# Running layer 0 of the next sequence beside the last layers of this one, in one block of an eight-layer kernel

## Chip, cores and metric

The kernel runs on one core of a Trainium2 chip. The metric is the device time of one execution in microseconds (us), taken as the median of several runs. TensorE is called PE here, VectorE DVE, ScalarE ACT, GpSimd POOL and SyncE SP; SP issues the DMAs.

## The reference

A float32 input of 8 sequences of 512 tokens with 128 features goes through eight residual layers, each on the layer norm of x:

```
x += mamba(ln(x))          # layer 0: silu(conv), x_proj, delta = softplus(...), both directions
                           # h = exp(delta*A)*h + delta*xc*B ;  y = sum_n h*C   (16 states n, 256 channels)
x += moe0(ln(x))           # 16 experts, grouped top-2, silu
x += attn1(ln(x)); x += lora1(ln(x)); x += attn2(ln(x))
x += block2(ln(x))         # attention, then ln, 8 experts of 512 with gelu, then ln
x += memory(ln(x))         # F = ret*F + coef*(v k^T) ;  y = (W_LTM + F) q, 8 groups of 128 rows
x += moe3(ln(x))           # 8 experts of 256: silu(h1)*h3, top-2 of softmax gates
```

A "sequence" is one pass over one of the 8 rows of the batch; all the weights stay in SBUF.

## The kernel before

`Fori(0, 8)` loops over the sequences. Its body is a row of stages, and each stage is one or more blocks. In a block every engine has its own in-order instruction list, with semaphores between the lists; at a block's end all engines meet. `norm_tiles` is a block of its own in front of each stage. SP clears the semaphores of finished stages in the next norm block, and those of the loop's last stage in a block of its own behind it.

Mamba has two blocks behind its norms. The first (the "pre" part) makes the projections, the convolutions (DVE), silu, delta by Abs, Exp and Ln (ACT), and the three-part bf16 rows `bcs` of B and C. The second is the scan: 32 steps (2 directions of 16 states), each over two tiles of channels at once, 1024 columns. In step s PE spreads the row of B over 128 partitions (L835), DVE multiplies it by `du` (L893) and one step later runs the scan (L900), ACT writes the decays into PSUM (L872) and copies the spread row of C (L878), POOL multiplies by C (L926), and PE adds the product of step s-4 into the accumulator with four matmul instructions (L849). DVE may not start the product of step s before that accumulation: `if s >= RW: dve.wait_ge(acc, s - RW + 1)`. The scan's PSUM use is 4 banks of decays, 2 of accumulators and 2 of spread rows.

`block2` ends in the experts of 512 (32 tiles of 128 hidden features: one up product, L1463, a gelu, L1488, one down product, L1454, and at each fourth tile `weigh`, L1502). They go round in 4 banks. `moe3` has 16 tiles; a tile has an up product (L1463), a gate product (L1465), a silu on ACT (L1492), one multiplication on DVE (L1512), and a down product. Up and gate products have two banks each. `memory` makes q, k and v parts, and then runs 8 groups, each with an outer product (L1692), a scan (L1694) and a read-out (L1700) on DVE, over two sets of three banks. `gates` makes the router's top-2 weights on DVE; its bank is `PS[7]`.

## Time and profile before

| what | us |
|---|---|
| median of 3 runs | 6054.27 |
| lowest and highest | 6046.32, 6057.73 |
| profiled execution, its own time | 6033.15 |
| span of that execution | 6031.4 |
| mean granted TensorE clock | 0.844 |
| busy: PE, DVE, ACT, POOL | 4418.4, 3707.3, 2786.1, 1094.8 |
| start of the second pass, start of the third | 798.66, 1546.12 |

A busy share of the whole span is a mean over stages with different limits, so it must be read stage by stage. The second pass of the loop, from 798.7 to 1546.1 us, is used for that. Durations of instructions in the rows are in us; the idle time of an engine before an instruction and what ended it stand in square brackets behind it.

### The profile page before, as it was taken

To read this page: it belongs to the slowest core of one execution; us is meant where nothing else is said; L and a number is where in the kernel's file an instruction comes from. 1 tells how busy PE (TensorE), PEld (TensorE's weight loads), DVE (VectorE), ACT (ScalarE), POOL (GpSimd) and SP (SyncE) were. 2 spreads that over 40 slices of the span, in tenths; PEclk is the share of its full clock that TensorE was granted. 3 is DMA by queue.
4 is the path that set the end of the run, shared out by engine and by line. 5 is a ranking of instruction groups with operands and counts; after the bars stand their busy time and mean duration, and the time that the engine had idled before them with its cause. 6 is when DMAs were issued, how large, how long until landed. Compare 5 with 4: busy or idle time off the path is not lost. (4 is left out here: it accounts for less than half of the span.)

```text
span 6031.4 us, 66197 instructions
## 1 busy us (share of the span) xinstructions
PE 4418.4 (73%) x20516; PEld 2189.1 (36%) x20516; DVE 3707.3 (61%) x8373; ACT 2786.1 (46%) x5281; POOL 1094.8 (18%) x1100
## 2 busy tenths in 40 slices
PE   5787767877678775787758877587775877758777
PEld 2342423424234242342424424243342433414334
DVE  6756477564775647756476554765548655486554
ACT  3455334553445534455344553455534555345553
POOL 2301033010330103301032010320104201042100
PEclk8987889878898788987889878898788987889778
DMA  2000000000000000000000000000000100001000
GB/s 109 19 31 1 2 3 25 25 1 2 3 25 25 1 2 3 31 19 1 2 3 31 19 1 2 3 31 19 1 2 3 37 13 1 2 3 37 13 1 4
DMA packets 30363, 84.02 MB, mean 14 GB/s; under 512 B 2640, under 2 KB 11856, under 8 KB 29440
## 3 DMA queue, kind: packets, MB, share of 16 engines
q1 hardware_dynamic: 29968, 79.30, 4.1%
q8 instruction: 182, 2.98, 0.2%
q14 instruction: 213, 1.74, 0.1%
HBM read 77.12 MB, written 2.16 MB: 13 GB/s over the span
## 5 line engine op out<-in xcount | busy, mean ns | idle before, releaser
L167 POOL TENSOR_TENSOR rstd<-rstd,WF 128x4 f32<-128x4 f32 x88 | 88.9, 1010 | 3692.8 <-DVE rstd L185 3005.2
L926 POOL TENSOR_TENSOR mamba_work<-mamba_work,mamba_c_all 128x1024 f32<-128x1024 f32 x256 | 602.4, 2354 | 324.6 <-DVE mamba_work L900 324.6
L900 DVE TENSOR_TENSOR_SCAN mamba_work<-BANKS,mamba_work 128x1024 f32<-128x1024 f32 x256 | 582.6, 2278 | 0.0
L835 PE MATMUL BANKS<-mamba_bcs,WB 96*128 96x512 bf16 x512 | 207.1, 414 | 427.2 <-DVE mamba_work L893 317.9
L849 PE MATMUL BANKS<-mamba_work,WF 128*128 128x512 f32 x1024 | 495.7, 607 | 17.5 <-POOL mamba_work L926 17.5
L1463 PE MATMUL BANKS<-XT,WF 128*128 128x512 f32 x768 | 418.5, 630 | 0.0
L1232 DVE CUSTOM_DVE_ANT_0 attn_biased<-BANKS,attn_toep 128x512 f32<-128x512 f32 x512 | 350.4, 685 | 55.0 <-DMA attn_toep<-bias_line 38.1
L1211 ACT COPY attn_probt<-BANKS 128x512 f32<-128x512 f32 x512 | 298.6, 583 | 168.3 <-PE BANKS L1137 165.3
L1203 ACT ACTIVATE attn_prob<-attn_biased,attn_nmax 128x512 f32<-128x512 f32 x512 | 373.7, 730 | 1.5 <-DVE attn_nmax L1232 1.4
L513 DVE TENSOR_REDUCE inner_nmax<-BANKS 128x1 f32<-128x512 f32 x512 | 322.5, 684 | 73.9 <-PE BANKS L386 71.3
L878 ACT COPY mamba_c_all<-BANKS 128x512 f32<-128x512 f32 x256 | 150.1, 586 | 428.7 <-PE BANKS L835 414.0
L893 DVE TENSOR_TENSOR mamba_work<-BANKS,mamba_du 128x1024 f32<-128x1024 f32 x256 | 313.0, 1223 | 40.1 <-PE BANKS L849 13.5
L872 ACT ACTIVATE BANKS<-mamba_delta,WF 128x511 f32<-128x511 f32 x512 | 334.0, 689 | 6.1 <-DVE mamba_work L900 6.0
L224 ACT COPY XT<-BANKS 128x256 f32<-128x256 f32 x64 | 23.8, 373 | 676.4 <-PE BANKS L216 676.4
L1137 PE MATMUL BANKS<-WF,attn_prob 128*128 128x128 f32 x2048 | 320.5, 281 | 8.8 <-ACT attn_probt L1211 4.9
L1137 PEld LDWEIGHTS BANKS<-WF,attn_prob 128*128 128x128 f32 x2048 | 218.4, 140 | 278.9 <-DVE attn_prob L1239 179.6
L1454 PEld LDWEIGHTS BANKS<-WF,block_a 128*128 128x128 f32 x2048 | 273.2, 195 | 124.3 <-issue 114.7
L510 DVE CUSTOM_DVE_ANT_0 attn_masked<-BANKS,WF 128x384 f32<-128x384 f32 (+3 forms) x512 | 231.1, 489 | 139.4 <-PE BANKS L386 138.4
L1502 DVE SCALAR_TENSOR_TENSOR block_Y<-BANKS,block_comb,block_Y 128x128 f32<-128x128 f32 x256 | 72.1, 344 | 380.0 <-PE BANKS L1454 380.0
L1488 ACT ACTIVATE block_a<-BANKS,WF 128x512 f32<-128x512 f32 x256 | 176.0, 687 | 264.9 <-PE BANKS L1463 264.8
L1130 PE MATMUL BANKS<-attn_qk 64*128 64x512 f32 x1024 | 289.0, 641 | 5.4 <-ACT attn_qk L1185 5.4
L835 PEld LDWEIGHTS BANKS<-mamba_bcs,WB 96*128 96x128 bf16 x512 | 48.5, 99 | 670.8 <-DVE mamba_work L893 497.2
(412 smaller groups left out, 9142.6 us busy)
## 6 DMA issues: line engine op xcount, KB each, us to landing
attn_toep<-bias_line SPq DMA_DIRECT2D x128, 448.0 KB, 4.4
WF<-in_wf SPq DMA_DIRECT2D x4, 1964.0 KB, 16.2
WF<-in_wf SPq DMA_DIRECT2D x3, 800.0 KB, 16.1
WF<-in_wf SPq DMA_DIRECT2D x3, 785.5 KB, 5.9
XIN<-in_x SPq DMA_DIRECT2D x9, 256.0 KB, 4.0
out<-X SPq DMA_DIRECT2D x8, 256.0 KB, 2.4
WF<-in_wf SPq DMA_DIRECT2D x1, 799.5 KB, 19.0
WF<-in_wf SPq DMA_DIRECT2D x1, 784.5 KB, 9.7
```

What stands on the lines that cost most here:

```text
L513: V.tensor_reduce(nmax[:, j, h:h + 1], bank("S", s), AX.X, ALU.max, negate=True).then_inc(maxed, 1)
L849: last = nc.tensor.matmul(PS[ACC + t][:, :], ident, work[:, m % RW, t, :], start=(n == 0), stop=(n == NS - 1))
L872: last = nc.scalar.activation(decay[m % RD][:, t, 1:], delta[:, d, t, 1:], ACT.Exp, scale=W("A")[:, a:a + 1])
L893: V.tensor_tensor(work[:, s % RW, :, :], bc(PS[SPREAD].unsqueeze(1), [P, ND, SEQ]), du[:, s // NS, :, :], ALU.mult).then_inc(drv, 1)
L900: V.tensor_tensor_scan(w, decay[m % RD].rearrange("p t s -> p (t s)"), w, 0.0, ALU.mult, ALU.add).then_inc(scn, 1)
L926: nc.gpsimd.tensor_tensor(work[:, m % RW, :, :], work[:, m % RW, :, :], bc(c_all[:, m % 2, :].unsqueeze(1), [P, ND, SEQ]), ALU.mult).then_ ...
L1130: nc.tensor.matmul(PS[(s + a) % NS_], q[:, j * P:(j + 1) * P], k, start=True, stop=True).then_inc(scored, 1)
L1137: last = nc.tensor.transpose(bank[:, kt * P:(kt + 1) * P], prob[:, u % NP_, kt * P:(kt + 1) * P], ident)
L1203: nc.scalar.activation(prob[:, e % NP_, :], biased[:, e % NS_, :], ACT.Exp, bias=nmax[:, e:e + 1], scale=-1.0, accum_out=den[:, e:e + 1]). ...
L1211: nc.scalar.copy(probt[:, u % NT_, :], RING[n % 2]).then_inc(freed, 1)
L1232: V.tensor_tensor_reduce(biased[:, s % NS_, :], PS[s % NS_], toep[:, h % 4, c:c + SEQ], -1.0, BIG, ALU.add, ALU.min, nmax[:, s:s + 1]).the ...
L1463: last = nc.tensor.matmul(PS[i % NB][:, :], w_up[:, i * P:(i + 1) * P], XT[:, :], start=True, stop=True)
```

## The change

The loop body starts with layer 1. Layer 0 of the first sequence runs alone ahead of the loop (stage `first`). In passes 1 to 7 the block `slot` runs layer 0 of the next sequence beside the second half of block2 (its norm and experts), memory and moe3 of this one; the last sequence is written out behind the loop, without a companion. Mamba has banks 0 to 3 and the three layers banks 4 to 7. Each layer is a Python generator for each engine: before a piece of work it yields the time in a plan at which that piece is due, and `in_turn` writes the pieces of both streams into one engine's list in the order of the due times. At run time only this order remains.

```
def in_turn(*streams):
    due = [next(s, None) for s in streams]
    while any(t is not None for t in due):
        i = min((t, i) for i, t in enumerate(due) if t is not None)[1]
        due[i] = next(streams[i], None)
```

Due times of mamba: pre part from 13.5, scan step s at `49.0 + 3.6*s` on PE, its tile t on DVE at `49.6 + 3.6*(s + t/2)`, its decays on ACT at `45.4 + 3.6*s`, the end from 164.2. Due times of the others: tile i of the experts of 512 at `7.6 + 2.0*i` (its gelu 1.0 later, the down product of tile i-1 also 1.0 later), second norm 73, norm of memory 79, memory 84 and its group g at `102 + 3.2*g`, norm of moe3 131, its tile i at `136.7 + 3.0*i`, the last piece at 187.7.

```diff
 # mamba scan, DVE (one step was: product of 1024 columns, then the scan of 1024 of the step before)
+                    if i:
+                        dve.wait_ge(scn, i)
+                    V.tensor_tensor(DRIVE, SPREAD, du[:, d, t, :], ALU.mult).then_inc(drv, 1)
+                    dve.wait_ge(drv, i + 1)
+                    dve.wait_ge(dec, i + 1)
+                    V.tensor_tensor_scan(work[:, s % RW, t, :], decay[:, s % RD, t, :], DRIVE, 0.0,
+                                         ALU.mult, ALU.add).then_inc(scn, 1)
 # C: rows go to DRAM once, and each step a DMA spreads one row
-                            spread(1, s - 1).then_inc(c_cast, 1)
-                        nc.scalar.copy(c_all[:, m % 2, :], PS[SPREAD + 1][:, :]).then_inc(c_cp, 1)
+                sp.dma_start(c_dram[d], rows_bc[NS:2 * NS, d, :]).then_inc(cput, 16)
+                if m >= RC:
+                    sp.wait_ge(rd, m - RC + 1)
+                src = bass.AP(row.tensor, row.offset, [[0, P], [1, SEQ]])
+                sp.dma_start(c_all[:, m % RC, :], src).then_inc(c_ld[m % RC], 16)
 # mamba pre part, ACT: both halves of softplus come off the bank, which the two directions share
+                nc.scalar.activation(soft[:, d, :, :], BANKS[:, 2:4, :], ACT.Abs).then_inc(ab, 1)
+                nc.scalar.activation(delta[:, d, :, :], BANKS[:, 2:4, :], ACT.Relu).then_inc(relued, 1)
 # mamba pre part, PE: the second direction
+                    pe.wait_ge(relued, 1)
 # moe3: silu(u)*g = (tanh(u/2)+1) * g/2 * u; up and gate products take turns in two banks
-                            nc.scalar.activation(s1[:, i % 2, :], PS[i % NB][:, :], func, bias=b_up[:, i:i + 1]).then_inc(acted, 1)
-            V.scalar_tensor_tensor(a1[:, i % 3, :], PS[2 + i % NB][:, :], b_gate[:, i:i + 1], s1[:, i % 2, :],
+                    nc.scalar.activation(s1[:, i % 2, :], UP[slot["up", i] % 2], ACT.Tanh, bias=half[:, i:i + 1],
+                                         scale=0.5).then_inc(acted, 1)
+                    act.wait_ge(hid, 2 * i + 2)
+                    nc.scalar.activation(g1[:, i % 2, :], UP[slot["gate", i] % 2], ACT.Identity, bias=half[:, n + i:n + i + 1],
+                                         scale=0.5).then_inc(gate_off, 1)
+                    link(V.scalar_tensor_tensor(s1[:, i % 2, :], s1[:, i % 2, :], 1.0, g1[:, i % 2, :], ALU.add, ALU.mult))
+                    V.scalar_tensor_tensor(a1[:, i % 3, :], UP[slot["up", i] % 2], b_up[:, i:i + 1], s1[:, i % 2, :],
+                                           ALU.add, ALU.mult).then_inc(gated, 1)
 # the loop
-    with nc.Fori(0, out.shape[0]) as b:
+    with Stage("first", last=True) as st:
+        layer = mamba(st)
+        with nc.Block() as block:
+            run(block, layer)
+        with Stage("slot", last=True, at_end=store) as st:
+            taken = st.sem("x_taken")
+            streams = [mamba(st, after=(taken, 1))] if ahead else []
+            streams.append(last_layers(st, taken))
+    with nc.Fori(0, out.shape[0] - 1) as b:
+        layers(b, True)
+    layers(out.shape[0] - 1, False)
```

Memory's groups have one set of three banks in place of two, and the experts of 512 two banks in place of four. Up product i of moe3 waits for the multiplication of tile i-1, which reads the bank. The slot has 123 semaphores (47 of mamba), cleared in a block behind it. The four middle stages and the first half of block2 stay.

## Rows read from the trace of the kernel before

**Rows 1.** Windows of pass two: us, busy us of PE, PEld, DVE, ACT, POOL; clock, DMA.

```profile
798.70:844.70 46.00, 21.18 (x37) 6.42 (x37) 32.43 (x65) 18.10 (x22) 8.20 (x8) 0.69 0.00 1
844.70:959.60 114.90, 73.66 (x183) 26.96 (x183) 110.54 (x66) 58.04 (x97) 74.41 (x32) 0.94 0.00 0
959.60:973.50 13.90, 7.75 (x24) 4.84 (x24) 5.01 (x8) 0.00 (x0) 2.50 (x2) 0.76 0.00 0
973.50:1356.20 382.70, 304.87 (x1644) 141.71 (x1644) 228.41 (x684) 213.51 (x456) 47.79 (x93) 0.83 0.06 20
1356.20:1427.30 71.10, 63.10 (x344) 45.75 (x344) 17.98 (x65) 24.34 (x36) 1.02 (x1) 0.93 0.00 1
1427.30:1438.80 11.50, 1.24 (x4) 0.75 (x5) 7.58 (x30) 0.37 (x1) 2.01 (x2) 0.51 0.00 1
1438.80:1457.40 18.60, 10.21 (x57) 6.89 (x58) 10.23 (x21) 11.85 (x18) 0.00 (x0) 0.66 0.00 1
1457.40:1484.90 27.50, 17.45 (x48) 6.66 (x48) 21.50 (x26) 6.80 (x10) 0.00 (x0) 0.89 0.00 0
1484.90:1540.00 55.10, 49.12 (x216) 31.05 (x216) 27.60 (x78) 14.62 (x21) 1.01 (x1) 0.90 0.02 6
1540.00:1546.10 6.10, 0.00 (x0) 0.00 (x0) 0.00 (x0) 0.00 (x0) 0.00 (x0) 0.52 0.17 51
```

**Rows 2.** Timeline of one scan step: start, us, engine, line, operation.

```profile
903.74 1.22 DVE L893 TENSOR_TENSOR mamba_work<-BANKS,mamba_du 128x1024 f32<-128x1024 f32 x1
904.88 2.28 DVE L900 TENSOR_TENSOR_SCAN mamba_work<-BANKS,mamba_work 128x1024 f32<-128x1024 f32 x1
905.02 0.39 PE L835 MATMUL BANKS<-mamba_bcs,WB 96*128 96x512 bf16 x1 [1.17 <-DVE mamba_work L893]
905.25 1.88 PE L849 MATMUL BANKS<-mamba_work,WF 128*128 128x512 f32 x4
...
907.24 1.22 DVE L893 TENSOR_TENSOR mamba_work<-BANKS,mamba_du 128x1024 f32<-128x1024 f32 x1
```

**Rows 3.** Timeline of one group of memory on DVE.

```profile
1461.48 0.68 DVE L1692 TENSOR_TENSOR memory_heb<-BANKS,memory_vrc 128x512 f32<-128x512 f32 x1
...
1462.20 1.23 DVE L1694 TENSOR_TENSOR_SCAN memory_mem<-WF,memory_heb 128x512 f32<-128x512 f32 x1
...
1463.46 0.75 DVE L1700 SCALAR_TENSOR_TENSOR memory_red<-memory_mem,WF,BANKS 128x512 f32<-128x512 f32 x1
```

**Rows 4.** Timeline of one tile of the experts of 512, on PE.

```profile
1406.26 1.05 PE L1454 MATMUL BANKS<-WF,block_a 128*128 128x128 f32 x8
...
1407.15 1.02 PE L1463 MATMUL BANKS<-XT,WF 128*128 128x512 f32 x2
...
1408.01 1.05 PE L1454 MATMUL BANKS<-WF,block_a 128*128 128x128 f32 x8
```

**Rows 5.** Timeline of moe3 on ACT, two tiles.

```profile
1505.63 0.69 ACT L1492 ACTIVATE moe_s<-BANKS,WF 128x512 f32<-128x512 f32 x1 [2.34 <-PE BANKS L1465]
...
1508.24 0.69 ACT L1492 ACTIVATE moe_s<-BANKS,WF 128x512 f32<-128x512 f32 x1 [1.92 <-PE BANKS L1465]
```

**Rows 6.** Timeline of ACT at the first gelu, behind the router's exponent.

```profile
1366.07 1.28 ACT L1488 ACT_TABLE_LOAD   x1
1367.36 0.69 ACT L1488 ACTIVATE block_a<-BANKS,WF 128x512 f32<-128x512 f32 x1
```

**Rows 7.** Timeline of ACT in the first stage: an Exp, then a Tanh.

```profile
47.41 0.19 ACT L671 ACTIVATE WF<-init_m_c 128x8 f32<-128x8 f32 x1
47.51 0.19 ACT L672 ACTIVATE init_m_t<-init_m_t 128x8 f32<-128x8 f32 x1
```

**Rows 8.** Timeline: the Abs of mamba's pre part.

```profile
826.71 1.01 ACT L754 ACTIVATE mamba_soft<-BANKS 128x1024 f32<-128x1024 f32 x1
```

**Rows 9.** The clearing line on SP, at moe0's norm and at the loop's end.

```profile
L143 SPq EVENT_SEMAPHORE_RANGE_CLEAR  x42: 25/30/35, 973.3 to 976.1; - x42
...
L143 SPq EVENT_SEMAPHORE_RANGE_CLEAR  x19: 25/30/37, 1540.6 to 1542.1; - x19
```

**Rows 10.** The page's DMA issues: KB each, median us to landing.

```profile
attn_toep<-bias_line SPq DMA_DIRECT2D x128, 448.0 KB, 4.4
```

More of the change, by code:

```diff
@@ L135, in clear_stale, with _ @@
     def clear_stale(block, first=lambda sp: None):
-        if stale:
-            @block.sync
-            def _(sp):
-                first(sp)
-                for stage in stale:
-                    for s in stage.sems:
-                        sp.sem_clear(s)
+        @block.sync
+        def _(sp):
+            first(sp)
+            for stage in stale:
+                for s in stage.sems:
+                    sp.sem_clear(s)
     def release_stale():
@@ L287, in weights @@
             beside(0)
+            yield 3.0
             score = ex
@@ L323, in gates @@
         pieces.products, pieces.turn, pieces.exponents, pieces.move, pieces.weights = products, turn, exponents, move, weights
-        pieces.combed, pieces.moved = combed, moved
+        pieces.combed, pieces.moved, pieces.shifted = combed, moved, shifted
         return pieces
@@ new lines, in run, with _ @@
+    def run(block, *streams, first=lambda sp: None):
+        @block.sync
+        def _(sp):
+            first(sp)
+            in_turn(*(p.sync(sp) for p in streams if "sync" in p.engines))
+        @block.tensor
+        def _(pe):
+            in_turn(*(p.tensor(pe) for p in streams))
+        @block.scalar
+        def _(act):
+            in_turn(*(p.scalar(act) for p in streams))
+        @block.gpsimd
+        def _(pool):
+            in_turn(*(p.gpsimd(pool) for p in streams))
+        @block.vector
+        def _(dve):
+            in_turn(*(p.vector(dve) for p in streams))
@@ L930, in bass_mk_seq, with layers, load_next @@
+    with Stage("first", last=True) as st:
+        layer = mamba(st)
+        with nc.Block() as block:
+            run(block, layer)
+    def layers(b, ahead):
+        def load_next(sp):
+            sp.wait_ge(x_free, 16)
+            sp.sem_clear(x_free)
+            sp.sem_clear(xin_ld)
+            if ahead:
+                sp.dma_start(XIN[:, :, :], one(xs, b + 1)).then_inc(xin_ld, 16)
         with Stage("moe0") as st:
-            norm_tiles(st, "ln", X, XN, XT)
+            norm_tiles(st, "ln", X, XN, XT, beside=load_next)
@@ L1008, in _ @@
                     V = nc.vector
-                    gate.weights(dve)
+                    for _ in gate.weights(dve):
+                        pass
                     link = Chain(dve, pch)
@@ L1273, in _ @@
                 def _(dve):
-                    gate.weights(dve)
+                    for _ in gate.weights(dve):
+                        pass
                     link = Chain(dve, ch)
@@ L1706, in store @@
-        def store(sp):
-            sp.dma_start(one(ys, b), X[:, :, :]).then_inc(x_free, 16)
-            sp.wait_ge(loaded, 16)
-        with Stage("moe3", last=True, at_end=store) as st:
-            loaded = st.sem("loaded")
-            def load_next(sp):
-                sp.dma_start(XIN[:, :, :], one(xs, b + 1)).then_inc(loaded, 16)
-            norm_tiles(st, "ln", X, XN, XT)
-            comb, comb_t = st.sb("comb", [P, NJ, E3]), st.sb("comb_t", [E3, SEQ])
-            gate = gates(st, XT, W("Wg3"), E3, comb, comb_t, eps=0.0)
-            experts(st, gate, W("W1_3"), W("W3_3"), W("b1_3"), W("b3_3"), W("W2_3"), W("b2_3", E3), E3, HID // P, ACT.Silu,
-                    comb, comb_t, X, load=load_next)
+        with Stage("attn3") as st:
+            norm_tiles(st, "ln", X, XN, XT)
+            O = st.sb("O", [P, NJ, D])
+            rope_attention(st, W("qkv3"), W("bqkv3"), True, False, O)
+            project_back(st, "pb", O, W("o3"), XN, bias=W("bo3"))
@@ new lines, in store, with clear @@
+        def store(sp):
+            sp.dma_start(one(ys, b), XO[:, :, :]).then_inc(x_free, 16)
+        def clear(sp):
+            for stage in stale:
+                for s in stage.sems:
+                    sp.sem_clear(s)
+        with Stage("slot", last=True, at_end=store) as st:
+            taken = st.sem("x_taken")
+            streams = [mamba(st, after=(taken, 1))] if ahead else []
+            streams.append(last_layers(st, taken))
+            with nc.Block() as block:
+                run(block, *streams, first=clear)
+            release_stale()
```

1197 lines of the change are left out of this document (709 added, 488 removed).

## The prediction

> **What bounds the kernel now.** I read the windows of the second pass first [rows 1], because the page's shares (PE 73%, DVE 61%) hide that the stages are bound in turn. The reader is to see that mamba's scan is DVE's (110.5 of 114.9 us), the experts of 512 and moe3 are PE's (63.1 of 71.1, 49.1 of 55.1), memory's groups are DVE's (21.5 of 27.5), and the rest is latency: in mamba's pre part DVE is busy for 32.4 of 46.0 us, in its tail (13.9) and in the norms (11.5) nobody is. Outside the middle stages (382.7) a pass takes 174.8 (mamba) + 183.8 (the three layers) + 6.1 (store, clearing, jump) = 364.7 us, and 8 of them are 2917.6. Then I read single steps in the timeline [rows 2 to 6] for the loops that come back in another form.
>
> **The room.** Beside each other the streams ask of DVE: mamba without its scan window 148.0 - 110.5 = 37.5; the scan as 64 pairs of product and scan of 512 columns. Such a pair stands in [rows 3]: from the outer product to the read-out 1.98, so 126.7. The three layers' DVE rows [rows 1] add up to 84.9, and moe3's second multiplication, priced as the read-out (0.75), adds 16 x 0.75 = 12. With 1.4 for emptying the accumulator that is 262 us against 358.6 in series. PE has 243.7 busy in the same rows, less 32 spreads of 0.39, much of it at a clock of 0.69. So DVE is the floor.
>
> **Part 1, layer 0 alone, once.** In the old step the accumulation is hidden: from the product's end (904.96) over spread and accumulation to the next product (907.24) is 2.28, the time of the scan [rows 2]. Now the wait starts at the second half's product, and only its scan of 1.26 covers it. A step is 1.98 + 0.70 + 2.28 = 4.96; the first four accumulate nothing and take 3.96; emptying costs 2. So 4 x 3.96 + 28 x 4.96 + 2 = 156.7 for 114.9, +42. Relu of 1024 columns (as Abs, 1.01 [rows 8]) lies partly on the pre part's path: +1. 174.8 + 43 = 217.8.
>
> **Part 2, three layers alone, once.** A tile of moe3 takes 2.61 [rows 5]. Now up product i waits for the multiplication of tile i-1: product 1.02 [rows 4], Tanh 0.69, Identity 0.69, two operations of DVE 1.5, five hand-offs together 0.35: 4.25. Fifteen tiles cost 15 x 1.64 = +24.6, and the router's comparisons, which now lie in that loop, +3. The experts of 512 keep PE's 1.75 per tile [rows 4] with two banks, since a gelu of 0.69 ends under the down product of 1.05. Memory +1, blocks merged -3. 183.8 + 25.6 = 209.4.
>
> **Part 3, clearing.** 42 clears took 2.8 us and 19 took 1.5 [rows 9], about 66 ns each. The slot's 123 lie between two blocks where nothing runs: 8.1 for 1.5, so an end of 12.7 for 6.1. The first stage has 47 (+3.1), the last 76 (end 9.9).
>
> **Part 4, C by DMA.** It takes 32 spreads (0.39 of PE) and 32 copies off ACT, neither of which was on the path, and puts 256 KB on SP's queue each step. Nothing here shows a spreading DMA; the nearest, 448 KB, lands in 4.4 us [rows 10], the small end is about nothing. The buffer is free two steps ahead, 8 to 10 us less POOL's 2.4, so I price it at 0; beyond 5 to 7 us it would be waited for. The decays written to SBUF and the product written to PSUM I take at the old durations.
>
> **Part 5, the slot.** I wrote down each engine's order from the due times and walked through it with the durations above, each piece starting when its engine is free and its last input is there. The four stretches:
>
> A, up to the first scan step: 84 us. The pre part alone has 46.0, and 20 of 32 tiles of the experts should ride along (20 x 1.75 = 35, below 46). But ACT must do both streams in one list. The list alternates exponent, gelu, silu, gelu, silu, gelu, silu, gelu, exponent, logarithm, gelu: at each change of function the trace has a load of 1.28 with nothing behind it [rows 6]. Additions to 46.0: +10 up to the last convolution (the inner norm's transposes stand on PE behind the first down product, which waits for the first gelu; DVE waits in the first `weigh` for the fourth down product); +13 to its silu (it stands on ACT behind the forward rows and gelus 8 to 11, and gelu 8 behind the forward rows of mamba; PE meanwhile waits in down product 8); +7 to the deltas (x_proj of the second direction waits for the Relu, which stands behind gelu 13, as the two directions share banks 2 and 3); +8 to the first product (two Relus, loads, and down product 19 stands before the first spread while its gelu stands behind decays that wait for delta). In series these parts took 46.0 plus about 46 for the norm and 20 tiles. So almost nothing is won. Unknown here is whether silu and gelu need a load between them, since the trace never has one behind the other: without it six loads (8 us of ACT) go, half of them in a chain, so A lies between 79 and 90 with PE's clock at the lower level for part of it.
>
> B, from there to memory's norm: 64 us for 9.5 steps and 12 tiles, in series 33 + 21 + 11.5 = 66. While gelus and decays alternate, a step needs of ACT 2 x 1.28 + 2 x 0.65 + 1.8 x 0.69 = 5.2, and the down product waiting for a gelu stands before the next spread: about 6 us a step.
>
> C, memory: 110 us for 14 steps, the 46.1 of its rows and a norm. DVE has 28 pairs (55.4) and 38 more; 17 are waits, of which 5.4 where PE stands in the wait for the last total's copy (ACT) with the next spread behind it, 3 where the first step waits behind memory's projections, 2 at the emptied accumulator. In series this was 14 x 3.5 + 46.1 + 5 = 100: DVE was nearly full in both parts before, and the pairs of 1.98 and the waits are added to it.
>
> D, moe3 with 8 steps and mamba's tail: 98 us. DVE has 16 pairs (31.7), 39.6 of moe3 and 5 of the tail. The tile loop of 4.25 and the step loop of 4.96 go through the same PE list, so a step in a tile's way costs both. The bad case: the multiplication of tile i-1 ends at 0; DVE goes on with a pair (its product ends at 0.7); PE does up and gate product of tile i until 1.9 and only then spread and accumulation, until 4.0; DVE's next pair runs from 4.1 to 6.1, and only behind it, in the order of the list, the two multiplications of tile i, ready since 2.8, until 7.6. In the good case the spread falls behind the down product and a tile takes 5.5, without a step 4.3. Seven tiles run behind the scan's end, the tail between them, at 4.25 and the tail's pieces, 38 us. In series D was 8 x 3.5 + 13.9 + 55.1 = 97.
>
> S = 84 + 64 + 110 + 98 = 356, as good as the 358.6 in series.
>
> **Sum.** Outside the middle: 217.8 + 3.1 + 209.4 + 9.9 + 7 x (S + 12.7) = 529.1 + 7 S, against 2917.6. Break-even is S = 341.2. With 356: +103.5. The profiled execution took 6033.15 (span 6031.4), which gives 6137; the median of the three runs lies 21 above it, 6054.27, so the forecast is 6158.
>
> One rule bears on it. The Trainium skill, "ScalarE: Activation LUTs", section "What ACT_TABLE_LOAD costs", gives 1.28 us for a load and 1.38 of drain behind it, and section "Rules for kernel authors" asks to do all of one table set before switching. The trace agrees with the load and not with the drain: the gelu starts 0.01 us after the load's end [rows 6]. With the page's drain the 27 loads of stretches A and B would cost 37 us more of ACT per slot.
> The page also has Exp and Tanh in one set ("Table sets: the hidden batching unit"), and the trace agrees, as no load stands between them [rows 7].
>
> **Rivals.** (1) The streams do fill each other's gaps, and the slot is the DVE floor with a start and an end that are half idle: 262 + about 50 = 312, that is -205, 5850. For it: in each stretch the three other engines are half idle; it decides below S = 341. Against it: my walk, and the single banks DRIVE, VB, KB and QB. It ends on the other side. (2) The waits feed on each other more than in a walk without any jitter, or PE's clock falls in its waits (0.69 in the old pre part, 0.94 in the scan [rows 1]): S = 385, +306, 6360. (3) Each change of function costs ACT more than its load, such as a wait for the pipe to empty before it. From the rows the gap is 0.01; doubled loads, of which some 23 lie in a chain, would give S = 385 too, 6360. (4) The gains of some stretches and the once-only costs cancel: S = 341 +- 2, 6054. (5) The change doesn't do what it says: the streams stand in series because one list waits for the other all through, S = 359 + 47 (steps) + 26 (moe3) = 432, +635.
>
> **How the numbers follow.** Forecast (S 344 to 372, 6073 to 6270): 0.50. Rival 1 (S 280 to 339): 0.28. Rival 2: 0.12. Rival 3: 0.03. Rival 4: 0.05. Rival 5: 0.02. About 0.2%, 12 us, is what a measurement of this kernel tells from no change, and S 339.5 to 343 is that. Faster 0.29, same 0.04, slower 0.67. To hold 8 in 10 the range takes in the forecast, the upper part of rival 1 (S from 325, -114) and rival 2 up to S = 385: 5940 to 6330, a little less than its end. The forecast's own range is 6073 to 6270.
>
> **What the profile should show.** From the slot's first norm to its last add about 356 us, DVE busy for about 260 of them (0.73); the first scan product 84 us after its start; 30 table loads in a slot, 9 in a pass before; single-stream steps of 4.96 in the stage ahead of the loop and moe3 tiles of 4.25 behind it; 123 clears in about 8 us; no wait for the DMAs of C. I am wrong if the slot is shorter than 341, and then I expect the error in stretch A, where the order is worst by my walk, or in D. A wait of POOL for C, or a product into PSUM over 0.7, would lengthen every step.

## The result, and the profile after

The changed kernel takes 6340.19 us (median of 4 runs, 6334.26 to 6347.79), the kernel before on the same chip 6052.22: a ratio of 1.0477, 95% interval 1.0459 to 1.0495. It is slower, as forecast, but by 288 us where the forecast had 104, and its time lies above the end of the range (6330). The profiled execution took 6347.79 us (span 6346.1, mean granted clock 0.820 for 0.844).

Windows of the changed kernel: the stage where layer 0 runs alone; 98.3 us of its scan; the first half of the first pass (the four middle stages and the first half of block2); then the first slot in the four stretches A, B, C, D of the prediction, and the whole of it; last, the last pass's three layers. A ends at the slot's first scan product, B at the last copy of memory's norm, C at the last copy of moe3's norm, in this kernel and in all the edits of it. Columns as in [rows 1].

```profile
51.10:324.80 273.70, 144.66 (x212) 49.02 (x212) 163.80 (x201) 62.83 (x89) 85.08 (x40) 0.60 0.10 31
101.70:200.00 98.30, 50.94 (x67) 16.66 (x68) 61.36 (x65) 23.90 (x36) 39.34 (x17) 0.53 0.16 46
324.80:711.90 387.10, 310.10 (x1644) 143.24 (x1644) 228.37 (x683) 213.40 (x456) 47.68 (x93) 0.82 0.07 21
...
711.90:796.10 84.20, 60.95 (x256) 36.53 (x257) 46.93 (x113) 48.66 (x62) 10.83 (x9) 0.88 0.03 8
796.10:858.20 62.10, 41.85 (x163) 23.67 (x162) 48.01 (x85) 38.33 (x46) 23.22 (x11) 0.83 0.13 38
858.20:982.60 124.40, 71.62 (x181) 31.06 (x182) 100.08 (x121) 38.88 (x57) 34.64 (x16) 0.79 0.09 30
982.60:1085.50 102.90, 75.67 (x282) 41.88 (x281) 74.57 (x119) 31.33 (x49) 21.78 (x9) 0.95 0.06 18
711.90:1085.50 373.60, 250.10 (x880) 133.15 (x880) 269.59 (x437) 157.20 (x211) 90.47 (x44) 0.86 0.08 23
...
6124.90:6340.20 215.30, 147.27 (x668) 93.14 (x668) 96.43 (x236) 68.03 (x100) 4.04 (x4) 0.85 0.00 0
```

The reader is to see three things. A (84.2) and B (62.1) came out as forecast (84, 64); C and D did not (124.4 for 110, 102.9 for 98). The seven slots take 373.6, 370.6, 373.5, 370.2, 370.6, 373.5 and 373.6, 372.2 on the mean, so a difference of 3 us in one slot says little. The first stage, which occurs once, is 273.7 us for a forecast of 217.8 + 3.1. And the first half of the pass, whose code the change leaves alone, has the 1644 matmuls of [rows 1] at 310.1 us of busy PE for 304.9.

A scan step of the first stage, in the timeline (answers to [rows 2]). The whole step, from one first product to the next, is 188.65 - 181.79 = 6.86 us. Most of the 28 steps that accumulate have this length; the next one, in which the accumulation takes 2.54, has 5.60.

```profile
181.79 0.70 DVE L899 TENSOR_TENSOR BANKS<-BANKS,first_du 128x512 f32<-128x512 f32 x1 [2.92 <-PE BANKS L745]
182.53 1.22 DVE L902 TENSOR_TENSOR_SCAN first_work<-first_decay,BANKS 128x512 f32<-128x512 f32 x1
183.78 0.70 DVE L899 TENSOR_TENSOR BANKS<-BANKS,first_du 128x512 f32<-128x512 f32 x1
184.52 1.22 DVE L902 TENSOR_TENSOR_SCAN first_work<-first_decay,BANKS 128x512 f32<-128x512 f32 x1
184.54 0.61 PE L735 MATMUL BANKS<-first_bcs,WB 96*128 96x512 bf16 x1 [2.84 <-DVE BANKS L899]
184.94 3.62 PE L745 MATMUL BANKS<-first_work,WF 128*128 128x512 f32 x4
188.65 0.70 DVE L899 TENSOR_TENSOR BANKS<-BANKS,first_du 128x512 f32<-128x512 f32 x1 [2.92 <-PE BANKS L745]
```

DVE's part is as forecast (product 0.70, scan 1.22). The four accumulating matmuls take 3.62 us where [rows 2] has 1.88: TensorE runs at its lower level of 1.2 GHz. The window says the same: a granted clock of 0.53.

The end of a slot, the clearing line on SP (answers to [rows 9]), and the page's DMA issues for C (the nearest rows were [rows 10]):

```profile
L149 SPq EVENT_SEMAPHORE_RANGE_CLEAR  x123: 25/30/43, 1086.6 to 1094.0; - x123
```

```profile
slot_c_all<-c_rows SPq DMA_DIRECT2D x224, 256.0 KB, 3.1
```

What ended DVE's waits in the slot, in the list of waits: us in total, times, longest.

```profile
DVE BANKS L899 <- PE BANKS L745: 34.5, 14, 8.8
DVE slot_bcs L863 <- ACT slot_rows_bc L762: 11.5, 2, 8.7
DVE slot_x_s L1044 <- ACT slot_x_g L1023: 9.8, 6, 2.9
DVE BANKS L899 <- PE BANKS L735: 8.3, 2, 6.0
DVE slot_Y L1033 <- PE BANKS L973: 7.9, 2, 7.1
```

The largest item is the scan's product waiting for PE, with the accumulation (L745) just ahead of its release. No wait names a DMA of C.

A group of memory in the slot (answers to [rows 3]), with POOL's multiplication beside it:

```profile
902.68 0.67 DVE L1234 TENSOR_TENSOR slot_heb<-BANKS,slot_vrc 128x512 f32<-128x512 f32 x1
...
902.84 2.35 POOL L829 TENSOR_TENSOR slot_work<-slot_work,slot_c_all 128x1024 f32<-128x1024 f32 x1 [3.95 <-DVE slot_work L902]
...
903.38 2.90 DVE L1238 TENSOR_TENSOR_SCAN slot_mem<-WF,slot_heb 128x512 f32<-128x512 f32 x1
```

Memory's scan, 1.23 in [rows 3], takes 2.90 here: it starts 0.54 us behind POOL's instruction, POOL ends at 905.19, and 1.1 us later, at 906.28, the scan is over. Mamba's scan (L902), which reads one operand from PSUM, takes 1.22 beside POOL as well.

### The profile page after: what moved, and what is told of

Read it like the earlier page. It is cut to its first block and busy times, and to the rows that moved or that the text cites. A ratio compares the mean times of both kernels' runs of the same rounds, so it can differ in the third digit from the quotient of the medians.

```text
span 6346.1 us, 66283 instructions
## 1 busy us (share of the span) xinstructions
PE 4553.8 (72%) x20260; PEld 2242.5 (35%) x20260; DVE 3996.1 (63%) x9013; ACT 2945.0 (46%) x5323; POOL 1102.1 (17%) x1100
## 5 line engine op out<-in xcount | busy, mean ns | idle before, releaser
L829 POOL TENSOR_TENSOR slot_work<-slot_work,slot_c_all 128x1024 f32<-128x1024 f32 x224 | 536.5, 2395 | 1199.0 <-DVE slot_work L902 1199.0
L808 ACT ACTIVATE slot_decay<-slot_delta,WF 128x512 f32<-128x512 f32 x448 | 298.8, 714 | 658.9 <-DVE slot_work L902 633.6
L902 DVE TENSOR_TENSOR_SCAN slot_work<-slot_decay,BANKS 128x512 f32<-128x512 f32 x448 | 546.6, 1220 | 15.3
L745 PE MATMUL BANKS<-slot_work,WF 128*128 128x512 f32 x896 | 539.4, 736 | 20.4 <-DVE slot_du L908 20.4
L899 DVE TENSOR_TENSOR BANKS<-BANKS,slot_du 128x512 f32<-128x512 f32 x448 | 310.6, 693 | 324.2 <-PE BANKS L745 233.2
L973 PEld LDWEIGHTS BANKS<-WF,slot_x_a 128*128 128x128 f32 x2688 | 368.4, 201 | 269.2 <-ACT slot_x_a L1015 142.1
L495 ACT ACTIVATE attn_prob<-BANKS 128x512 f32<-128x512 f32 (+3 forms) x896 | 401.1, 532 | 129.0 <-PE BANKS L397 125.2
L973 PE MATMUL BANKS<-WF,slot_x_a 128*128 128x128 f32 x2688 | 381.7, 288 | 86.1 <-ACT slot_x_a L1015 86.1
L397 PE MATMUL BANKS<-attn_parts_kT,attn_parts_qT 64*128 64x512 bf16 (+3 forms) x896 | 314.2, 444 | 32.6 <-ACT attn_parts_qT L475 20.7
L524 DVE TENSOR_REDUCE attn_nmax<-BANKS 128x1 f32<-128x512 f32 x448 | 282.0, 683 | 71.2 <-PE BANKS L397 68.9
L745 PEld LDWEIGHTS BANKS<-slot_work,WF 128*128 128x128 f32 x896 | 208.7, 235 | 195.7 <-issue 184.4
```

The source lines that it names most:

```text
L397: nc.tensor.matmul(bank(kind, i), left[rows, P * tile:P * (tile + 1)], right[rows, lo:hi], start=True, stop=True).then_inc(sem, 1)
L495: nc.scalar.activation(prob[:, i % PR, lo:hi], bank("T", i), ACT.Exp).then_inc(exped, 1)
L745: last = nc.tensor.matmul(PS[t][:, :], ident, work[:, m % RW, t, :], start=(n == 0), stop=(n == NS - 1))
L808: nc.scalar.activation(decay[:, m % RD, t, :], delta[:, d, t, :], ACT.Exp, scale=W("A")[:, a:a + 1]).then_inc(dec, 1)
L829: nc.gpsimd.tensor_tensor(work[:, m % RW, :, :], work[:, m % RW, :, :], bc(c_all[:, m % RC, :].unsqueeze(1), [P, ND, SEQ]), ALU.mult).then ...
L899: V.tensor_tensor(DRIVE, SPREAD, du[:, d, t, :], ALU.mult).then_inc(drv, 1)
```

## The experiments

All are edits of the changed kernel (6340) unless said otherwise. The slot and its stretches are of the first pass, except where the mean of the seven slots is given; a pass is the time from moe0's norm to that of the next sequence, 773.3 in the changed kernel's first pass. A single run is given without an interval. The kernel before took 6034 to 6055 beside them, so some 20 us of a difference between two single runs can be noise.

Slots in us, from the first statistics to the last addition:

| run | first slot | mean of seven |
|---|---|---|
| changed kernel | 373.6 | 372.2 |
| acc_first (2) | 355.5 | 355.5 |
| tables (4) | 363.4 | 363.8 |
| poolcut (5) | 367.7 | 368.1 |
| hebps (6) | 373.8 | 367.7 |
| yev (7) | 373.2 | 370.9 |
| silu (8) | 359.3 | 357.3 |
| combo (9) | 334.5 | 334.4 |
| combo_slow (10) | 333.9 | 335.0 |
| combo_fast (11) | 341.1 | 340.9 |
| zeros1, zeros2 (13, 14) | 373.1, 375.1 | 375.4, 375.9 |
| combo_zeros (15) | 339.7 | 339.1 |

**1. The streams in series.**

```diff
             with nc.Block() as block:
-                run(block, *streams, first=clear)
+                run(block, streams[-1], first=clear)
+            if ahead:
+                with nc.Block() as block:
+                    run(block, streams[0])
```

> Same instructions as the changed kernel, but the slot's two streams stand in two blocks one behind the other, the three layers first, mamba second. Theory (the overlap itself works, and the rewritten forms and the once-only parts eat it): the new forms cost alone what the stage ahead of the loop (273.7 us) and the last pass's three layers (215 us) take, so a slot grows from 371 to about 488 us, the run to about 6340 + 7 x 117 = 7160 us. Rival (the shared lists make the streams wait for each other so much that beside and behind each other cost the same): about 6340 us.

Measured: 7133.68. Windows of the three layers and of layer 0, first pass:

```profile
712.60:927.90 215.30, 147.78 (x668) 93.13 (x668) 96.25 (x236) 67.99 (x100) 4.05 (x4) 0.85 0.00 1
927.90:1197.90 270.00, 144.79 (x212) 48.99 (x212) 163.62 (x201) 62.84 (x89) 84.91 (x40) 0.58 0.10 31
```

In series the new forms need 485 us (215.3 + 270.0); one block brings them to 373.6. So the streams do overlap, by about 112 us a pass, and the fifth rival is out. But the old forms took 358.6 in series [rows 1]: the new forms cost 127 before they save anything, and 95 of that is layer 0 (270.0 for 174.8), at a clock of 0.58.

**2. The accumulation ahead of the spread.** The product of step s needs the spread of s, but not the accumulation of s-4.

```diff
 # the pieces cut at "..." are moved, not changed
             for s in range(STEPS + AHEAD):
-                yield SCAN + STEP * s if s < STEPS else TAIL + 1.0 + s - STEPS
+                m = s - AHEAD
+                if m >= 0:
+                    yield SCAN + STEP * s - 1.2 if s < STEPS else TAIL + 1.0 + s - STEPS
+                    ...                       # accumulation of step m
                 if s < STEPS:
+                    yield SCAN + STEP * s
                     ...                       # spread of step s
-                m = s - AHEAD
-                if m >= 0:
-                    ...                       # accumulation of step m
```

> The accumulation of step s-4 stands on PE ahead of the spread of step s (due 1.2 earlier), not behind it; nothing else changes. Theory (the path product, spread, four accumulating instructions, next product sets the step, and its waits let PE's clock fall): a step alone goes from 6.86 to about 4.0 us, the stage ahead of the loop from 274 to about 185, and of the 34.5 us that DVE waits for the accumulation in a slot some 25 go: 6340 - 88 - 175 = about 6080 us. Rival (in the slot the wait only moves to another piece of the lists): about 6250 us.

Measured: 6143.01, between the theory's 6080 and the rival's 6250. The first stage is 204 us (-69; the theory had 185), the step 4.08, the pass 756.1 (-17). Windows of the scan alone, then of A to D:

```profile
101.70:200.00 98.30, 55.41 (x104) 19.44 (x105) 88.65 (x94) 31.93 (x48) 54.10 (x23) 0.78 0.19 62
...
643.40:727.70 84.30, 61.18 (x256) 36.71 (x257) 46.90 (x113) 48.66 (x62) 10.83 (x9) 0.88 0.02 8
727.70:783.10 55.40, 41.72 (x164) 23.99 (x164) 48.60 (x86) 38.23 (x46) 23.25 (x11) 0.84 0.13 41
783.10:899.70 116.60, 69.38 (x183) 29.64 (x181) 99.52 (x121) 38.12 (x57) 34.64 (x16) 0.78 0.11 33
899.70:998.90 99.20, 75.59 (x279) 42.34 (x279) 73.71 (x120) 31.22 (x49) 21.76 (x9) 0.93 0.06 19
```

A stays. B loses 6.7, C 7.8 and D 3.7, although C now holds 15 steps for 14 (and D 7 for 8), and the clock is no higher in C and D (0.78 for 0.79, 0.93 for 0.95); so in the slot the gain is the order's. In the first stage order and clock come together: the clock is 0.78 for 0.53. The place of four matmuls in a list is worth 197 us, two thirds of the whole regression.

**3. TensorE kept busy in the first stage.** Two products behind each accumulation, into banks unused there. The other pieces of the edit, which pass `warm=True` to the first stage alone, are left out.

```diff
+                    if warm and s < STEPS:
+                        for k in range(2):
+                            nc.tensor.matmul(PS[6 + k], ident, W("early"), start=True, stop=True)
```

> In the stage ahead of the loop only, two float32 products of 512 columns into unused banks follow each accumulation, in the time in which PE would wait for the next product of DVE. Theory (the step of 6.86 us there, forecast at 4.96, is the forecast's path at half the clock): granted clock of the stage's scan from 0.56 to above 0.9, step about 5.0, stage 274 to about 218, the run 55 us shorter. Rival (the step is another chain, such as POOL or the DMA of C): stage unchanged or longer.

Measured: 6302.27, 38 us shorter where 55 were expected; the first stage is 227 us (-46), for 218. Window and step (the first product at 149.36 and 154.30):

```profile
101.70:200.00 98.30, 66.06 (x149) 26.32 (x150) 77.08 (x81) 28.16 (x43) 47.96 (x21) 0.90 0.18 56
```

```profile
152.10 0.39 PE L735 MATMUL BANKS<-first_bcs,WB 96*128 96x512 bf16 x1 [1.12 <-DVE BANKS L902]
...
152.33 1.88 PE L745 MATMUL BANKS<-first_work,WF 128*128 128x512 f32 x4
```

With more work PE is faster: clock 0.90, accumulation 1.88, step 4.94. That is the forecast's step of 4.96, so the order was priced rightly and the clock was not. What still lies above 217.8 is in part the emptied accumulator, whose step takes 9.23 in place of 4.95: 4.3 us for the 2 of the forecast.

**4. The gelu of the experts of 512 and the silus of mamba as Tanh.** The output changes; only the functions differ, so that table loads go. Both stand in the slot, and in the first stage and the last pass too.

```diff
-                nc.scalar.activation(zs[:, t, :], PS[ND + t][:, :], ACT.Silu).then_inc(zed, 1)
+                nc.scalar.activation(zs[:, t, :], PS[ND + t][:, :], ACT.Tanh).then_inc(zed, 1)
...
-                    nc.scalar.activation(xc[:, d, t, :], xc[:, d, t, :], ACT.Silu).then_inc(silu, 1)
+                    nc.scalar.activation(xc[:, d, t, :], xc[:, d, t, :], ACT.Tanh).then_inc(silu, 1)
...
-                    nc.scalar.activation(a1[:, i % 3, :], UP[slot["up", i] % 2], ACT.Gelu, bias=b_up[:, i:i + 1]).then_inc(acted, 1)
+                    nc.scalar.activation(a1[:, i % 3, :], UP[slot["up", i] % 2], ACT.Tanh, bias=b_up[:, i:i + 1]).then_inc(acted, 1)
```

> The gelu of the experts of 512 and the silus of mamba's pre part are Tanh (other values), so that they need no other table than Exp; the table loads in a slot fall from 30 to about 8. Theory (the loads lie in the chain of stretches A and B): both together shrink from 146 to about 128 us, the run to about 6340 - 7 x 18 = 6214 us. Rival (ACT has room beside PE and DVE there): within 12 us of 6340.

Measured: 6282.4, 58 us shorter for the theory's 126. The slot's table loads fall from 29 to 4, a pass is 763.7 (-9.6); A is 79.1 (-5.1), its ACT busy for 34.2 us in place of 48.7, as the window shows:

```profile
715.20:794.30 79.10, 61.69 (x255) 37.07 (x256) 46.93 (x113) 34.19 (x51) 10.83 (x9) 0.87 0.03 7
```

Loads count, but a third of ACT's saving arrives. The third rival, loads that cost double, would have put A far above 84.

**5. POOL multiplies 16 of 512 columns.** The output changes; POOL's instruction is all but gone.

```diff
-                nc.gpsimd.tensor_tensor(work[:, m % RW, :, :], work[:, m % RW, :, :],
-                                        bc(c_all[:, m % RC, :].unsqueeze(1), [P, ND, SEQ]), ALU.mult).then_inc(rd, 1)
+                nc.gpsimd.tensor_tensor(work[:, m % RW, :, 0:16], work[:, m % RW, :, 0:16],
+                                        bc(c_all[:, m % RC, 0:16].unsqueeze(1), [P, ND, 16]), ALU.mult).then_inc(rd, 1)
```

> POOL's product with C takes 16 columns of each tile in place of 512, so that most of y isn't multiplied by C; every wait stays. Theory (DVE operations with both operands in SBUF are held up while POOL multiplies in SBUF, as memory's scan, 1.22 us alone and 2.90 beside a product of POOL): DVE's busy time in a slot falls from 270 to about 250 us, memory's scan to 1.22 us, a slot by 12 to 18 us, the run to about 6340 - 105 = 6235 us. Rival (DVE's long operations come from something else, such as the DMAs of C): DVE's busy time unchanged, the run within 20 us of 6340.

Measured: 6312.23. Memory's scans, the slot's window and that of C:

```profile
L1238 DVE TENSOR_TENSOR_SCAN slot_mem<-WF,slot_heb x8: 1224/1224/1226, 903.0 to 954.5; 128x512 f32<-128x512 f32 x8
```

```profile
711.80:1079.50 367.70, 256.38 (x880) 137.16 (x880) 253.14 (x437) 157.19 (x211) 23.23 (x44) 0.82 0.08 23
858.40:978.30 119.90, 75.70 (x181) 33.23 (x182) 88.09 (x121) 38.81 (x57) 5.26 (x16) 0.71 0.10 31
```

In the changed kernel the same eight scans have a maximum of 2895 ns. With POOL gone DVE is busy for 253.1 in place of 269.6, so 16.5 us of DVE's busy time in a slot was waiting beside POOL. Twelve of them lie in C (88.1 for 100.1). The slot is only 5.9 shorter (4.1 on the mean of seven), and the expectation for the run was nearly four times as much. That speaks against DVE as the bound, but does not settle it: the clock fell as well (0.82 for 0.86 in the slot, 0.71 for 0.79 in C), and the same 181 matmuls of C took PE 4.1 us more, which can have hidden a part of the gain.

**6. Memory's outer product in place in PSUM**, so that its scan reads one operand from SBUF.

```diff
-                    pe.wait_ge(hd, g)
+                    pe.wait_ge(sd, g)
...
-                V.tensor_tensor(heb[:, :], KB, vrc[:, g % 2, :], ALU.mult).then_inc(hd, 1)
+                V.tensor_tensor(KB, KB, vrc[:, g % 2, :], ALU.mult).then_inc(hd, 1)
...
-                V.tensor_tensor_scan(mem[:, :], bc(W("ret")[:, g:g + 1], [P, SEQ]), heb[:, :], 0.0,
+                V.tensor_tensor_scan(mem[:, :], bc(W("ret")[:, g:g + 1], [P, SEQ]), KB, 0.0,
                                      ALU.mult, ALU.add).then_inc(sd, 1)
```

> Memory's outer product is written over its own PSUM bank, so that the scan reads one operand from PSUM, as mamba's does; PE's next product into that bank waits for the scan. Theory (both operands in SBUF): the scan has 1.22 us beside POOL too, 5 us less of DVE in a slot, the run 20 to 35 us shorter. Rival: the scan keeps its 1.85 us mean.

Measured: 6314.54. All eight scans take 1.22. The first slot is not shorter (373.8), the other six are, by 3.5 to 7 us. In the timeline the scan stands beside POOL's instruction (902.26 to 904.61):

```profile
902.80 1.22 DVE L1238 TENSOR_TENSOR_SCAN slot_mem<-WF,BANKS 128x512 f32<-128x512 f32 x1
```

**7. PE's wait for memory's last total 1.2 later in its list.**

```diff
             total(NG - 1)
+            yield G0 + STEP * NG + 1.2
             pe.wait_ge(yev, 1)
```

> PE's wait for the copy of memory's last total comes due 1.2 later, behind the next spread of mamba, not ahead of it. Theory (the wait of DVE for the accumulation there, 8.8 us in the first slot, is a wait behind a piece of the other stream): 6 us off a slot, the run 42 us shorter. Rival (memory's end is itself the chain): no change.

Measured: 6328.77. The spread now goes ahead, and DVE's longest wait falls from 8.8 to 6.0:

```profile
969.19 0.70 DVE L899 TENSOR_TENSOR BANKS<-BANKS,slot_du 128x512 f32<-128x512 f32 x1 [5.99 <-PE BANKS L745]
```

The first slot is only 0.4 us shorter (1.3 on the mean of seven), and the 11 us of the run are within the noise of single runs. Stretches C and D hold other waits of the same kind, and the time is given back there or in the order of the steps behind; where exactly was not located. A stall that the forecast had priced by itself (5.4) is not worth what it lasts.

**8. moe3 with Silu again:** one multiplication on DVE and no Identity on ACT, with the two banks as changed.

```diff
-                    nc.scalar.activation(s1[:, i % 2, :], UP[slot["up", i] % 2], ACT.Tanh, bias=half[:, i:i + 1],
-                                         scale=0.5).then_inc(acted, 1)
...
-                    nc.scalar.activation(g1[:, i % 2, :], UP[slot["gate", i] % 2], ACT.Identity, bias=half[:, n + i:n + i + 1],
-                                         scale=0.5).then_inc(gate_off, 1)
+                    nc.scalar.activation(s1[:, i % 2, :], UP[slot["up", i] % 2], ACT.Silu, bias=b_up[:, i:i + 1]).then_inc(acted, 1)
...
-                    link(V.scalar_tensor_tensor(s1[:, i % 2, :], s1[:, i % 2, :], 1.0, g1[:, i % 2, :], ALU.add, ALU.mult))
-                    V.scalar_tensor_tensor(a1[:, i % 3, :], UP[slot["up", i] % 2], b_up[:, i:i + 1], s1[:, i % 2, :],
+                    V.scalar_tensor_tensor(a1[:, i % 3, :], UP[slot["gate", i] % 2], b_gate[:, i:i + 1], s1[:, i % 2, :],
                                            ALU.add, ALU.mult).then_inc(gated, 1)
```

> moe3 with the Silu of ACT and one multiplication on DVE again, in two banks. The up bank is free after the Silu. Theory (the tile loop through two operations of ACT and two of DVE costs more than table loads): the last pass's three layers go from 215 to about 190 us, a slot loses 0 to 8 us although Silu and Exp take turns there, the run 25 to 80 us shorter. Rival (some 16 more table loads in a slot lie in the chain): the last pass gains the 25 us, a slot is longer by more than 5 us, the run longer than 6350 us.

Measured: 6209.31, more of a gain than expected. The last pass's three layers take 188 us for 215, the slot 359.3 for 373.6, although its table loads rise from 29 to 40. Stretch D alone falls from 102.9 to 85.7:

```profile
984.00:1069.70 85.70, 71.67 (x282) 40.22 (x281) 61.31 (x104) 35.14 (x44) 21.11 (x9) 0.99 0.07 22
```

The tile alone, in the timeline of the changed kernel and then of this one (answer to [rows 5]):

```profile
6292.09 0.69 ACT L1020 ACTIVATE zslot_x_s<-BANKS,HB 128x512 f32<-128x512 f32 x1 [2.79 <-PE BANKS L983]
...
6296.54 0.69 ACT L1020 ACTIVATE zslot_x_s<-BANKS,HB 128x512 f32<-128x512 f32 x1 [2.90 <-PE BANKS L983]
```

```profile
6169.31 0.69 ACT L1020 ACTIVATE zslot_x_s<-BANKS,WF 128x512 f32<-128x512 f32 x1 [1.92 <-PE BANKS L983]
6171.92 0.69 ACT L1020 ACTIVATE zslot_x_s<-BANKS,WF 128x512 f32<-128x512 f32 x1 [1.92 <-PE BANKS L983]
```

4.45 against 2.61: with Silu even two banks give the old tile. It is the Tanh form that holds a bank for two more operations.

**9. Edits 2, 6, 7 and 8 together** (combo), the one edit with more than one run.

> Four edits together on the changed kernel: the accumulation ahead of the spread in PE's list, moe3 with Silu and one multiplication, the wait for memory's last total 1.2 later in PE's list, and memory's outer product multiplied in place in PSUM. One by one they took 197, 131, 12 and 26 us off 6340. If they are independent the sum is 5975 (5950 to 6005), below the kernel before (6052): a slot of about 334 us, first stage 204, the last pass's three layers 188. Rival: the first two take the same waits of stretch D away (step and tile loop there share PE's list), so that together they bring at most the larger one in the slot: 6050 to 6080, no better than before.

Measured: 5972.28 (5971.14 to 5985.1) against 6034.4 of the kernel before: ratio 0.9902, interval 0.9885 to 0.9919. The first slot:

```profile
643.20:727.60 84.40, 61.24 (x256) 36.73 (x257) 46.98 (x114) 48.63 (x62) 10.82 (x9) 0.86 0.03 8
727.60:782.80 55.20, 41.47 (x164) 23.96 (x164) 48.55 (x86) 38.23 (x46) 23.21 (x11) 0.84 0.14 41
782.80:894.40 111.60, 68.07 (x183) 29.35 (x181) 94.71 (x122) 38.36 (x57) 34.64 (x16) 0.78 0.13 34
894.40:977.70 83.30, 71.90 (x279) 41.19 (x279) 61.24 (x103) 35.10 (x44) 21.07 (x9) 0.95 0.08 23
```

So the four mends make the change 1% faster than the kernel before, not slower. A slot is 334.5 us, below the forecast's break-even of 341.2. The four gains add up (197 + 131 + 11 + 26 = 365; measured 368), more closely than single runs can show. D is 20 us shorter than in the changed kernel.

**10 and 11. Combo with the scan steps due every 4.0 or every 3.3 us.**

> As combo, with mamba's scan steps due every 4.0 us in place of 3.6, so that more steps lie in moe3. Theory (each stretch is bound by waits in lists, not by DVE, and C is the fullest stretch of DVE while D has room): a slot 3 to 10 us shorter than in combo, 20 to 60 us in all. Rival: moe3's tiles are the chain of D, and each step put among them costs its 2 us of PE: slot longer by 5 or more, plus a tail that then lies bare: over +35 us against combo.

> As combo, with steps due every 3.3 us in place of 3.6 (more of them in the experts of 512 and memory, fewer in moe3). By the same theory C gets fuller and the slot 2 to 8 us longer, +15 to +55 us against combo; the rival says shorter by that.

Measured: 5995.92 and 6018.16, single runs. With 3.3 the slot grows by 6.5 us on the mean (340.9 for 334.4), which makes up the 46 us, as the theory said: C is fuller. With 4.0 the slot is not shorter, as the theory had it, nor longer by 5, as the rival had it (335.0 for 334.4); the 24 us lie mostly outside the slot, in stages that the edit leaves alone. The plan's 3.6 is near the best of these three.

**12. Combo in series.**

> As combo, but with the slot's two streams in two blocks one behind the other (the three layers first). It prices the overlap itself with the mended forms: mamba alone 204 and the three layers alone 188 make 392 and a block between, against a slot of 334 in combo: 5975 + 7 x 60 = 6395 (6350 to 6450). Rival: the clock, which is lower where the engines wait for each other, gives half of the overlap back when they don't: 6200 or less.

Measured: 6329.33. Windows of the three layers and of layer 0:

```profile
641.70:829.70 188.00, 143.32 (x668) 91.39 (x668) 85.82 (x220) 58.31 (x85) 4.05 (x4) 0.84 0.00 1
829.70:1028.10 198.40, 107.76 (x212) 38.74 (x212) 163.71 (x201) 61.79 (x88) 84.98 (x40) 0.78 0.14 43
```

386.4 in series, 334.5 beside each other: the overlap is worth 52 us here. Against the old form (174.8) the four-bank layer 0 still costs 24.

**13 to 15. Products with a matrix of zeros behind each accumulation,** in the first stage and the slots: one (zeros1), two (zeros2), and one in combo (combo_zeros).

```diff
                     last.then_inc(acc, 1)
+                    if n < NS - 1 and s < STEPS:
+                        for k in range(1):   # range(2) in zeros2
+                            nc.tensor.matmul(PS[k][:, :], W("early")[:, 0:P], W("early"), start=False, stop=False)
```

> One product with a matrix of zeros is added onto the accumulator after each step's accumulation, in the first stage and in the slot: the result stays, TensorE gets 0.94 us of work more per step at full clock. Theory (the falling clock made the first stage and part of stretches C and D long): clock up in both, first stage 225 to 240 in place of 273.7, slot 5 to 12 us shorter, 6220 to 6270. Rival (in the slot the clock is no matter, PE's list is): first stage as above, slot longer by up to 28 x 0.94 = 26 us where steps stand in PE's way, 6300 to 6480.

> As zeros1 with two such products (1.88 us per step at full clock). Theory: clock at 0.9 in the first stage as in warm (227), slot's clock higher again, but PE's list fuller: about zeros1, 6200 to 6290. Rival: slot longer than in zeros1 by 10 to 26 us, +70 to +180 against zeros1.

> One such product per step in combo. Step of the first stage from 4.08 towards 3.7 (first stage 204 to 192), slot between -6 (clock) and +10 (PE's list): 5915 to 6030 for combo's 5972. Theory says below 5972.

Measured: 6317.01, 6317.87 and 6013.07. The first stage falls by 33 and 45 us, as expected; but in combo, where the accumulation stands first, it does not (203.4 for 203.6, 192 expected): the step stays 4.08 although the clock of its scan rises from 0.78 to 0.87, as DVE's two pairs (3.96) now fill it. Stretch C of zeros2:

```profile
813.50:938.10 124.60, 85.92 (x233) 37.90 (x234) 99.52 (x121) 38.78 (x57) 34.69 (x16) 0.88 0.09 30
```

The clock in C rises from 0.79 to 0.88 and C stays (124.6 for 124.4). On the mean of seven the slots are 375.4 and 375.9 for 372.2, and combo's becomes 5 us longer; the runs came out as the rival of zeros1 had it (6300 to 6480), not as the theory. What the higher clock gives back, the added work on PE (1.9 us a step in zeros2) may take again, so that the clock is part of C's excess is neither shown nor excluded by this. What is excluded is that such filling work mends the slot.

## Why the prediction was right in its sign and wrong in its size

The forecast span was 6031.4 + 103.5 = 6134.9; the profiled one is 6346.1. The missing 211 us are, within 1: the first stage 53, seven passes of 773.1 on the mean for 356 + 12.7 + 382.7 = 751.4 (21.7 each, 152), the last pass 7. By stretch, on the mean of the seven slots (84.2, 62.3, 123.6, 102.1), the 152 are C 95, D 29, the first half of the pass 38, and B -12. So the steps that failed are three: Part 1's accumulation at full clock, Part 5's terms for C, and the first half of the pass, taken at its old time. That the change is slower at all is shown by experiment 1: its forms cost 127 us a pass and the overlap gives 112 back.

**Part 1 failed, by 53 us in a stage that runs once.** It built the step of 4.96 from an accumulation of 1.88 at full clock, as if the 0.94 of [rows 1] belonged to the scan and not to how PE was used there (73.7 us busy of 114.9). The new order leaves PE idle while DVE does both halves; the clock is 0.53, the accumulation doubles, and the step grows to 6.86, in which PE waits longer still. Experiment 3 restores 4.94 with the clock alone, and experiment 1 shows the same 270 us wherever layer 0 stands alone. The prediction held the clock as a rival for the slot (0.12), not for the stage where it does most. Experiment 2's order takes 69 away, the clock's rise to 0.78 with it, and the step of 4.08 that it leaves is the same at 0.87 (experiment 15).

**Part 2 held.** Tile mostly 4.34 to 4.45 for 4.25 (the first three 5.17 to 5.53), three layers 215.3 for 209.4 (+6). Experiment 8 takes 27 us back, which the tile alone explains (15 x 1.84 = 27.6); the +3 for the router's comparisons, which it leaves in place, is not shown by a run.

**Part 3 held.** From the slot's last addition to the next statistics 12.7 us, as forecast; 123 clears in 7.4 us, 60 ns each. (Its 66 ns fits the 42 clears of [rows 9], not the 19, which make 79.) The end of the last pass is 5.9 for 9.9.

**Part 4 held.** C's DMAs land in 3.1 us and nobody waits; product 0.70, scan 1.22.

**Part 5, A and B held** (84.2 for 84, 62.1 for 64), with 29 table loads in the slot on ACT for 30. The loads were a part of A's length (experiment 4: 5 us), and the gap behind a load stays that of [rows 6] where ACT's next input is there. The walk's other additions to A (10, 13, 7 and 8 us, in which waits and loads are mixed) were not measured one by one, so that 84.2 meets 84 may be luck in part. B's 62.1 is not a floor: the order of experiment 2 makes it 55.4.

**Part 5, C failed by 14.4.** Its term for DVE, 55.4 + 38 = 93.4, is 100.1 in the window, and its 17 us of waits are 24.3. The first is contention, shown by experiments 5 and 6: DVE's scans and products with two operands in SBUF stand still while POOL multiplies. Experiment 5 puts it at 12 us of C, as DVE is busy for 88.1 there without POOL; so the term without contention was 5 too high, and the two errors hid each other in part. The Trainium skill bears on it, "SBUF — State Buffer", section "Who interferes with whom": a DVE instruction with two SBUF inputs contends with a GpSimd instruction that reads SBUF, and the port pair that they share is an exclusive lock. The trace agrees (2.90 for 1.23, ending 1.1 us behind POOL's end), and mamba's scan with an operand in PSUM is untouched. [Rows 3] came from a stage without POOL, so the walk could not see this. The second is PE's order: with the accumulation ahead of the spread C has 116.6 - 99.5 = 17.1 us of waits, the number forecast, even with 15 steps for 14, and with memory's product in PSUM as well C is 111.6 for the forecast 110.

**Part 5, D failed by 5.** DVE's busy 74.6 is the forecast's 76.3; the waits are 28.3 for 21.7. Each of the two loops that share PE's list has its part: the shorter step alone takes 3.7 us off D (experiment 2), the shorter tile alone 17.2 (experiment 8), both 19.6 (combo). The forecast's "a step in a tile's way costs both" is in keeping with this; which waits it mis-sized was not isolated.

**Not foreseen: the first half of the pass,** 387.1 for 382.7 in the first pass and 388.2 on the mean. In the second pass it lies in two attention stages: attn1 takes 143.2 for 141.0, and the attention of block2 with its end 96.7 for 93.4, while moe0, lora1 and attn2 with their norms keep their times to 0.1. In both stages PE has the same count of matmuls and is busy longer by 2.2 and 3.0, which makes up nearly the whole, at a lower clock (0.96 for 0.98, 0.75 for 0.77). It is there in combo in series too, so the overlap is not its cause. Why the clock is lower there was not settled.

**The rivals.** The first (S = 312) is out; of its floor of 262, DVE is busy for 270, and for 253 without POOL. The second named the right thing and priced it at 385 for 372; within it, waiting that feeds on PE's order is shown, the clock only outside the slot. That its 6360 lies near the measured 6340 is luck: its slot is 13 us too long, seven times, and the first stage and the first half of the passes, which it left alone, make up for it. The third and fifth are out by experiments 4 and 1, the fourth by the result itself (the slots take 372, not 341). Experiment 5 speaks against DVE as the bound once more, with the clock's fall as the reservation: 16.5 us of it freed, 5.9 gained.

## What to carry to other kernels

Before two stages are put side by side, price the forms that sharing the banks forces on each of them alone: here they added 127 us to 358.6, which the overlap's 112 did not repay. In an in-order list put work that nobody waits for soon into the time when the engine waits anyway, ahead of the instruction whose input is late; moving one accumulation was worth 197 us. The price of a DVE instruction with both operands in SBUF, taken where POOL is idle, is a lower end for a stage where POOL multiplies beside it (1.23 became up to 2.90). And price a matmul at the clock of the stage as it will be, not as it was: if a change makes PE wait more, take the lower level as one end of the range: the four matmuls of 1.88 us took 3.62.

## What was unexpected of the hardware

- The clock and a dependent chain feed on each other: the steps that accumulate mostly take 6.86 us at 0.53 and, with 1.88 us more work for PE per step, 4.94 at 0.90. With the accumulation ahead of the spread the loop is broken: 4.08 at 0.78 and at 0.87.
- DVE's wait for POOL's instruction appears as busy time of the DVE instruction (1.23 to 2.90), not as idle time before it; in sum 16.5 us of a slot's 269.6.
- A spreading DMA of 256 KB per step, 3.1 us to landing, cost the scan nothing that the waits show: POOL, which reads what it brings, waits for DVE alone.
